# Last batch dense through both experts, first spread ahead of the weight pieces, tile choice and weight fetch ahead of the exponentials

## The reference

```python
x = x + xattn(layernorm(x), ctx, ctx)      # 16 batches of 256 tokens, 256 wide, 16 heads of 16
x = x + ffn(layernorm(x))

# xattn: blocks of 64 keys; every query block of the pattern has a softmax of its own,
# and the outputs of the blocks are added; then @ Wo.T
# ffn:
gate_scores = xf @ gate_w.T                # 2 experts, each token goes to one of them
one_hot = one_hot(argmax(softmax(gate_scores)), 2)
masked = xf[None] * one_hot.T[:, :, None]
h = relu(einsum('end,edh->enh', masked, w1) + b1[:, None, :])      # hidden 1024
expert_out = einsum('enh,ehd->end', h, w2) + b2[:, None, :]
shared = relu(xf @ sw1 + sb1) @ sw2 + sb2
return expert_out.sum(0) + shared
```

## Time and profile before

| | |
|---|---|
| median of 3 executions | 1091.39 us (1087.02 to 1092.59) |
| the profiled execution, own time | 1088.73 us |
| its span, first to last instruction | 1086.9 us |
| granted TensorE clock, mean | 0.924 of full speed |
| busy: PE / PEld | 81% / 68% |
| busy: DVE / POOL / ACT | 49% / 46% / 41% |
| DMA moved | 164.68 MB, mean 152 GB/s |

### The profile page before, as it was taken

One profiled execution on the slowest core, in us unless ns is written; L12 is line 12 of the kernel. 1 busy time (PEld: TensorE's weight loads), 2 busy tenths in 40 slices (PEclk: granted clock), 3 DMA queues, 4 the chain that ended last, 5 costly groups with the idle time before them and its releaser, 6 DMA issues. The chain is left out here.

```text
span 1086.9 us, 21971 instructions
## 1 busy us (share of the span) xinstructions
PE 880.9 (81%) x7654; PEld 734.8 (68%) x7654; DVE 535.5 (49%) x1089; ACT 444.3 (41%) x974; POOL 499.9 (46%) x816
## 2 busy tenths in 40 slices
PE   3377788889888898887998888889888799898564
PEld 2155566777767686776877686868677686768564
DVE  4467473464636464554736364545556373634100
ACT  3151524344444444353443444444445344344232
POOL 7242525154453536262543535363636344457333
PEclk8577887999999999999998999999999999999777
DMA  9666563819284655739192746647382909152740
GB/s 243 152 204 165 175 127 119 202 59 232 43 247 77 202 126 165 163 83 245 43 241 44 240 89 193 135 135 193 93 235 78 250 26 253 42 195 91 278 165 10
DMA packets 95745, 164.68 MB, mean 152 GB/s; under 512 B 9040, under 2 KB 81616, under 8 KB 87008
## 3 DMA queue, kind: packets, MB, share of 16 engines
q1 hardware_dynamic: 75552, 69.80, 29.4%
q10 hardware_dynamic: 9792, 71.31, 18.8%
q0 software_dynamic: 10368, 23.14, 8.4%
HBM read 124.30 MB, written 39.91 MB: 151 GB/s over the span
## 5 line engine op out<-in xcount | busy, mean ns | idle before, releaser
L1285 POOL TENSOR_TENSOR hl<-h,hh 128x256 fp32r<-128x256 f32 x264 | 197.3, 756 | 416.7 <-ACT hh L810 416.7
L990 DVE TENSOR_REDUCE nmax<-work 128x8 f32<-128x512 f32 x256 | 163.8, 684 | 101.5 <-PE work L468 101.5
L789 ACT ACTIVATE PT<-work 128x512 f32<-128x512 f32 x256 | 131.0, 611 | 80.4 <-PE work L483 80.4
L468 PE MATMUL work<-KP,QP 96*128 96x512 f32 x256 | 102.0, 477 | 74.6 <-DMA QP<-scratch_q 64.4
L810 ACT ACTIVATE h<-hid,bias 128x256 f32<-128x256 f32 x144 | 68.6, 476 | 191.1 <-PE hid L428 183.0
L483 PE MATMUL work<-QP,KP 128*128 128x256 f32 x512 | 104.3, 324 | 46.3 <-ACT PT L789 24.5
L996 DVE COPY T<-num 128x512 f32<-128x512 f32 x64 | 44.3, 692 | 189.0 <-PE num L501 189.0
L483 PEld LDWEIGHTS work<-QP,KP 128*128 128x128 f32 x512 | 74.5, 198 | 82.3 <-ACT PT L789 44.0
L428 PE MATMUL hid<-XS,WS 128*128 128x256 f32 x816 | 118.2, 296 | 3.1 <-DVE idle L1158 3.1
L428 PEld LDWEIGHTS hid<-XS,WS 128*128 128x128 f32 x816 | 109.6, 201 | 11.8 <-issue 6.2
L468 PEld LDWEIGHTS work<-KP,QP 96*128 96x128 f32 x256 | 46.3, 211 | 95.5 <-DMA QP<-scratch_q 43.6
(11 more groups left out here) (197 smaller groups left out, 1544.5 us busy)
## 6 DMA issues: line engine op xcount, KB each, us to landing
WR<-wx ACTq DMA_DIRECT2D x64, 1024.0 KB, 10.0
KP<-scratch_k SPq DMA_DIRECT2D x96, 128.0 KB, 12.4
QP<-scratch_q SPq DMA_DIRECT2D x96, 128.0 KB, 13.7
scratch_k<-T SPq DMA_DIRECT2D x16, 512.0 KB, 3.9
scratch_q<-T SPq DMA_DIRECT2D x16, 512.0 KB, 2.9
wx<-WR POOLq DMA_DIRECT2D x16, 512.0 KB, 3.9
stages<-wraw POOLq DMA_DIRECT2D x24, 256.0 KB, 5.7
rowin<-queue SPq DMA_DIRECT2D x16, 260.0 KB
```

The lines of the kernel that those rows point to most:

```text
L468: nc.tensor.matmul(bank, R(QP[0:SHIFT_ROW, p, P * t:P * t + P]), R(KP[0:SHIFT_ROW, p, :, :]), start=True, stop=True).then_inc(sem["s_full" ...
L789: nc.scalar.activation(PT[:, j % 8].rearrange("p t q -> p (t q)"), work[:, BANK[("st", j)], :], ACT.Exp).then_inc(sem["exp_done"], 1)
L990: nc.vector.tensor_reduce(nmax[:, t, 8 * p:8 * p + 8], work[:, BANK[("s", j)], :].rearrange("q (b k) -> q b k", k=BLOCK), AX_X, ALU.max, n ...
L1285: nc.gpsimd.tensor_tensor(R(hl[:, k % 2, a]), h32[:, k % 2, a], hh[:, k % 2, a], ALU.subtract).then_inc(sem["hl_done"], 1)
```

## The change

The queue holds 15 batches instead of 16. The last batch isn't appended: in the tail it goes through both experts whole, once with expert 0's rows kept and once with expert 1's, masked by `last_mask`, and both sums and the shared expert's stay in one PSUM accumulation, added to x1b at the end and stored by SP. In the tail stand now, in units: 1 to 3 of the 14th full tile, 4 of the rest of expert 1 (WX, XL1), 4 of the rest of expert 0 (WR, XL0), 4 of the last batch through expert 0 (WR, XD0), 4 through expert 1 (WX, XD1), 4 through the shared expert (WS, XS). WX is expert 1's weights in buffers that attention no longer needs (KP, QP, wp_hi), fetched by SP once; WR is refilled once with expert 0's. These are six passes: 23 calls of `ffn_up` and 24 of `ffn_down`.

In the loop, PE does `up(6)` behind the third transposed score tile instead of behind the last `values`, `up(7)` ahead of `spread_inverse`, and `down(7)` ahead of `project_out`. ACT fetches the weights ahead of the first exponential, in two DMAs of 2 MB, and does `relu(6)` behind the second group of exponentials. POOL does `update` and `select` ahead of `append`.

At the start, DVE clears QP, V is no longer used for spread_pairs, and POOL issues the pieces from the fifth on only once the first spread has landed.

```diff
-QROWS = BATCH * SEQ
+QROWS = (BATCH - 1) * SEQ
...
+        WX = [KP[:, 0:4].rearrange("p a b c -> p (a b c)"), KP[:, 4:8].rearrange("p a b c -> p (a b c)"),
+              QP.rearrange("p a c -> p (a c)"), wp_hi.rearrange("p a b c -> p (a b c)")]
+        XL1, XL0, XD0, XD1 = (c_hi, c_lo), (a_hi, a_lo), (wp_lo[:, 0], wp_lo[:, 1]), (wp_lo[:, 2], wp_lo[:, 3])
...
-            sp.wait_ge(sem["zeroed"], 7)
+            sp.wait_ge(sem["kp_zeroed"], 1)
+            sp.wait_ge(sem["qp_zeroed"], 1)
             spread(16, "first_q_bounced", "first_k_bounced")
...
             iteration(LAST, False)
-            load_tile(LAST + 1)
-            store(LAST + 1)
-            load_tile(LAST + 2)
+            sp.wait_ge(sem["sel_done"], LAST)
+            sp.wait_ge(sem["rT_full"], LAST - 1)
+            sp.wait_ge(sem["ids_done"], LAST - 1)
+            start = sp.value_load(control[0:1, 0:1], min_val=0, max_val=QROWS - TILE)
+            sp.dma_start(rowin[:, :, :], queue[bass.ds(start, TILE), :].rearrange("(t p) w -> p t w", p=P)) \
+                .then_inc(sem["row_loaded"], 16)
+            sp.wait_ge(sem["st_full"], HEADS * BATCH)
+            load_unit(WX[0], 1, 0, "wx_loaded0")
+            load_unit(WX[1], 1, 1, "wx_loaded0")
+            load_unit(WX[2], 1, 2, "wx_loaded1")
+            sp.wait_ge(sem["wo_full"], BATCH)
+            load_unit(WX[3], 1, 3, "wx_loaded2")
+            for k in range(RU):
+                sp.wait_ge(sem["w2_done"], unit_no(BATCH, k) + 1)
+                load_unit(WR[:, k], 0, k, f"wl_loaded{k}")
+            sp.wait_ge(sem["finished"], TAIL_PASSES[3])
+            sp.wait_ge(sem["routed_out"], 32 * LAST)
+            sp.dma_start(out[LAST].rearrange("(t p) d -> p t d", p=P), x1b[:, :, :]).then_inc(sem["out_done"], 16)
...
+            ffn_up(i, 1)
+            ffn_down(i, 0)
+            tail_tokens(0, xhat, 1)
+            ffn_up(i, 2)
+            ffn_down(i, 1)
+            tail_tokens(1, xin, 2)
...
+            for i in (BATCH + 1, BATCH + 2):
+                for k in range(UNITS):
+                    ffn_up(i, k)
+                    ffn_down(*((i, k - 1) if k else (i - 1, UNITS - 1)))
+            ffn_down(i, UNITS - 1)
...
-                for k in range(RU):
-                    if type(i) is not int or i > 2:
-                        act.wait_ge(sem["w2_done"], unit_no(i, k) + 1)
-                    act.dma_start(WR[:, k].rearrange("p a b c -> p (a b c)"),
+                for h in range(2):
+                    act.dma_start(WR[:, 2 * h:2 * h + 2].rearrange("p k a b c -> p (k a b c)"),
...
+            nc.vector.memset(QP[:, :, :], 0.0).then_inc(sem["qp_zeroed"], 1)
             norm1_stats(0)
...
+            dve.wait_ge(sem["w2_done"], unit_no(BATCH + 2, UNITS - 1) + 1)
+            dve.wait_ge(sem["x1b_done"], BATCH)
+            nc.vector.tensor_tensor(x1b[:, :, :], acc[:, :, :], x1b[:, :, :], ALU.add).then_inc(sem["finished"], 1)
...
-                    append(i - 1)
                     update(i - 1)
                 if type(i) is not int or i >= 2:
                     select(i - 1)
+                if later:
+                    append(i - 1)
...
+            pool.wait_ge(sem["k_spread"], 96)
+            pool.wait_ge(sem["q_spread"], 96)
+            for n in range(4, STAGES + EARLY_PIECES):
+                load(n)
...
+            pool.wait_ge(sem["routed_out"], 32 * (LAST - 1))
+            nc.gpsimd.tensor_copy(ids[:, :], rowin[:, :, D]).then_inc(sem["ids_done"], 1)
             hidden_low(i, 6)
...
             for t in range(TT):
                 pool.indirect_dma_start(out_rows, by_row(ap=ids[:, t:t + 1], axis=0), yr[:, t, :], None,
                                         compute_op=ALU.add).then_inc(sem["routed_out"], 16)
-            pool.wait_ge(sem["routed_out"], 32 * BATCH)
```

More of the change, by code:

```diff
@@ L55, in pass_no @@
     return 0 if type(i) is int and i == 1 else 2 * (i - 2) + (k >= RU)
+TAIL_PASSES = {n: pass_no(BATCH, 0) + n for n in (1, 2, 3)}
 def active(i, k):
@@ L600, in ffn_up @@
+                                       [(hi[:, c, :], lo[:, c, :]) for c in range(DC)])
                 mm.then_inc(sem["hid_full"], 1)
@@ L658, in iteration @@
                     front_project(i + 1, "q", 0, a_hi, a_lo, "xT_lo")
-                for j in range(4):
+                for j in range(3):
                     scores_t(i, j)
+                up(6)
+                scores_t(i, 3)
                 for v in range(VISITS):
@@ L714, in _ @@
-            nc.tensor.matmul(work[:, 1, 2:3], ones16[:, :], mask16[:, 1:2], start=False, stop=True,
-                             skip_group_check=True).then_inc(sem["cnt_full"], 1)
-            ffn_down(i, 2)
-            for k in range(RU, UNITS):
-                ffn_up(i, k)
-                ffn_down(i, k - 1)
-                if k == UNITS - 2:
-                    pe.wait_ge(sem["row_loaded"], 16 * LAST)
-                    transposed(work[:, 2], rowin).then_inc(sem["rT_full"], 1)
-            i = LAST + 2
@@ L735, in _ @@
-            i = LAST + 3
-            for k in range(RU):
-                ffn_up(i, k)
-                ffn_down(*((i, k - 1) if k else (i - 1, UNITS - 1)))
-            ffn_down(i, RU - 1)
+            transposed(work[:, 2], rows).then_inc(sem["x2T_full"], 1)
+            ffn_up(i, 4)
+            ffn_down(i, 3)
+            ffn_up(i, 5)
+            ffn_down(i, 4)
+            tail_tokens(0, ctx_in, 3)
+            ffn_up(i, 6)
+            ffn_down(i, 5)
+            tail_tokens(1, x1, 4)
+            ffn_up(i, 7)
@@ L1222, in _, with tail_low, masked @@
             halves = "p (c t) -> p c t"
-            norm2_apply(LAST)
-            gate_scores(LAST, 0)
-            gate_scores(LAST, 1)
-            choose(LAST)
-            shared_low(LAST, work[:, 0].rearrange(halves, c=2))
-            route(LAST, work[:, 1])
-            finish_routed(LAST + 1)
-            dve.wait_ge(sem["upd_done"], BATCH)
+            def tail_low(n, bank, dst):
+                low(n - 1, "tail_hi", work[:, bank].rearrange(halves, c=2), dst[0][:, :, :], dst[1][:, :, :], "tail_lo")
+            def masked(dst, src, which, e):
+                for t in range(TT):
+                    last = nc.vector.tensor_scalar(dst[:, t, :], src[:, t, 0:D], which[:, e, t:t + 1], None, ALU.mult)
+                last.then_inc(sem["tail_masked"], 1)
+            dve.wait_ge(sem["upd_done"], LAST)
             dve.wait_ge(sem["sel_done"], LAST)
@@ L1242, in _ @@
                 .then_inc(sem["left_step"], 1)
[L1243 to L1245 removed]
+            dve.wait_ge(sem["row_loaded"], 16 * LAST)
             dve.wait_ge(sem["left_step"], 4)
[L1247 to L1251 removed]
@@ L1523, in _ @@
             iteration(LAST, False)
-            i = LAST + 1
+            pool.wait_ge(sem["row_loaded"], 16 * (LAST - 1))
+            pool.wait_ge(sem["wr_loaded1"], 16 * (LAST - 1))
+            nc.gpsimd.tensor_copy(control[:, 0:1], head0[:, :]).then_inc(sem["sel_done"], 1)
+            i = BATCH
             reciprocal_deviation(LAST, 1)
-            hidden_low(i, 1)
+            for k in range(1, 4):
+                hidden_low(i, k)
             add_bias(LAST)
-            hidden_low(i, 2)
-            hidden_low(i, 3)
-            append(LAST)
-            update(LAST)
-            select(LAST)
             hidden_low(i, 4)
@@ L1561, in _ @@
                                         compute_op=ALU.add).then_inc(sem["routed_out"], 16)
-            pool.wait_ge(sem["routed_out"], 32 * BATCH)
+            for k in range(RU + 1, UNITS):
+                hidden_low(i + 1, k)
+            for k in range(UNITS):
+                hidden_low(i + 2, k)
 def kernel(**inputs):
```

271 lines of the change are left out of this document (128 added, 143 removed).

## The result

| | median of the runs, us | lowest to highest |
|---|---|---|
| before | 1091.99 | 1087.02 to 1100.73 (4 runs) |
| changed | 1113.03 | 1108.92 to 1115.21 (4 runs) |

The ratio is 1.020, its 95% interval 1.015 to 1.025: slower by 2%, where 990 us were forecast with a range to 1035. In some executions a kernel runs in a slower state, and runs over 1.5% above the fastest of the same kernel are left out of every median and ratio here. The profiled execution has a span of 1107.1 us against 1086.9.

The account below looks back on a forecast made before the run. PE and its wait for the spread, held up by the weight fetch, were taken to bound the loop. Loop -55 - 36 + 17 = -74, start -5, tail -19 from 1086.9, plus 1.8 outside: 991, stated as 990 us, range 962 to 1035.

Parts of the forecast that it names:

- (a): Loop: ACT issues the weight fetch 7.4 us sooner, so the spread needs its own time only; 55 us saved.
- Both losses, 43 and 12 us: Loop: PE's waits for the spread over 13 iterations, 43 us, and lower granted clock in six windows, 12 us; both go.
- R1: Rival, loop: the fetch collides with the row queue, rows land at 675 and the spread wait returns; 1029 us, chance 0.14.
- R4: Rival, loop: appended rows hold SP's one queue, the spread is issued 4.0 us later; 1123 us, chance 0.04.
- R5: Rival, loop: late control keeps the fetch from getting ahead; (b) lost, (a) half; 1038 us, chance 0.05.
- The rule that I held against (c): Loop DMA: engines alternate queues by packet, so appended rows would be in only with the weights, at 675.
- (c): Loop: rows appended later delay SP's tile fetch and PE's rowin; costs 1.3 us an iteration, 17 us, bounds 0 and 52.
- The chance of 0.05 for slower: Whole kernel: chance that the change makes it slower, from R4 at 0.04 and a little of mixtures.
- (b): Loop: up(6) among the transposed scores, up(7) and up(0) farther down, fill PE's waits; 2.4 us an iteration, 36 us saved.
- the layout by hand: Loop: PE's schedule with exponentials of 0.51 us; the last den group ends at 676.35 with up(6) done, 2.0 us gained.
- The start: Before the loop: fewer weight pieces issued into the first spread; 5 us saved, first scores at 31 to 35.
- The tail: Behind the loop: units, waits and the end take 87 us against 106; 19 us saved, bounds 8 and 27.

Follow-up runs that it names:

- e9: Changed kernel with the weight fetch at the same place, as four 1 MB transfers in 8 KB pieces instead of two of 2 MB in 16 KB; 1032.2 us.
- e1: Changed kernel with the weight fetch issued behind the first four exponentials instead of ahead of them; 1031.7 us, ratio 0.946 to before.
- e7: Changed kernel with the weight fetch issued behind one exponential instead of ahead of the first; 1017.9 us.
- e8: Changed kernel with the same two 2 MB weight transfers issued by SP behind its store of q, in one queue, instead of by ACT; 1013.1 us.
- e3: Changed kernel with the weight fetch at the same place, as four 1 MB transfers in 4 KB pieces instead of two of 2 MB in 16 KB; 1029.8 us.
- e11: Changed kernel with q's parts in their own tile instead of T's first half, four staging buffers instead of six, and an added ACT wait; 1033.9 us.
- e4: Kernel before with only its four 1 MB weight transfers moved ahead of the first exponentials; 1114.9 us, ratio 1.022 to before.
- e13: e7 with up(6) and its relu put back behind the products, as before the change; 1033.8 us.
- e2: Changed kernel with the weight fetch back at the third visit, its place before the change; 1097.8 us, ratio 1.005 to before.
- e14: e7 with append again ahead of update and select on POOL, as before the change; 1049.5 us.
- e15: e7 with the weight fetch of iteration 2 alone moved behind four exponentials; 1023.2 us.

## Why the prediction was wrong

**The step that failed.** Term (a) followed the fetch forward in time and asked what it would meet: the exponentials, the spread, the tile, the rows. It never asked what it would land on. "The weights are issued at 662.5" stands in the forecast; the kernel before issued its store of q at 662.10 in that iteration, so the two were 0.4 us apart on paper, with no row in the text for that store. In the changed kernel both follow the same copy of q and are 0.06 to 0.18 us apart, where at 0.34 to 0.37 us the store still lands in under 5 (table above). The sum also had the cut of the fetch as nothing but 0.47 us an issue; with the four transfers of the kernel before at the same place (e9) it takes 1032.2 us. "Both losses, 43 and 12 us, go" came true for the first: the spread's DMAs land 5.0 and 8.1 us after issue (forecast 6 to 9) and PE's wait for it is 2.5 us in the loop. In its place came the wait for T, 94.0 us of PE in 11 iterations, and the low clock, 0.92 to 0.95 in the windows of these. e1, e7 and e8 (fetch 1 to 3 us later, in e8 in the store's queue too: minus 81, 95 and 100 us), e3 and e9 (only the cut of the fetch: minus 83 and 81) and e11 (the tile and the waits for it: minus 79) show it from three sides.

**The rivals.** R1 and R4 had the right kind of mechanism, small rows beside large ones, on the wrong victim. R4's number, 1123, is near the result by accident: its mark, the spread issued late because of the rows, is not what bounds the changed kernel, where SP's spread waits for TensorE in 13 cases. R5 is what e4 shows, in the kernel before without the new order on POOL. The rule that I held against (c), turns between queues, spoke against (a); I applied it to one small transfer and not to all that are in flight at that moment. The chance of 0.05 for slower was far too small for an edit that puts 4 MB at a new place.

**(b)**, forecast at 36 us, is worth 11 to 16 (e13, up to 22 by the periods) where the fetch is out of the way, and 3 beside e1's fetch, which cannot be told from nothing; in e2, where the spread binds, it bought nothing. Of the 4.0 us of waiting an iteration that the layout by hand counted on, PE had 24.5 / 15 = 1.6 us as waits in the earlier trace rows; the rest I had taken for waits "between matmuls" without a row.

**(c)**, forecast at 17 us: in e7 PE waits 3.2 us for rowin and 23.5 - 14.9 = 8.6 us for the spread in the loop, 12 together; in e8 15.1 and 10.4. The size was about right, as waits; what the rows cost in time was not measured by itself. But the edit that has this price also makes control early, which is worth 26 to 32 us once the fetch is ahead (e14).

**The start**, forecast at 5 us: the first scores begin at 33.93, inside the 31 to 35, but by the fourth store of q 1.7 us are left (175.31 against 176.96), and none in e7. **The tail**, forecast at 87 us: 86.87, with one wait of PE of 3.03 us and one of 2.06, and 7.0 us from the last matmul (1100.1) to the end. Right in its parts too.

**The rest.** e7 is 28 us above the forecast. (b) explains 14 to 25 of them and the start 5, (c) gives 5 back, and the one stall left in e7 would be 8; e15 without that stall was not faster, so how these add up is not settled. e15's best period is 54.07, the forecast one; what makes others 58 is a wait of 2.5 us for the spread with a lower clock behind it. Why one iteration falls on this side and the next on the other stays open.

## What to carry to other kernels

When a transfer is moved, list every transfer that is issued within a few microseconds of its new place, with the buffer that each holds and who wants that buffer next; a small store with a reader nearby is the one to look for, not only the loads that the move is meant to help. If two must be issued together, put the small one first and leave a microsecond between them (e7: the store lands in 3.4 us), or cut the large one in smaller pieces (e3: 5.7). Moving the large one into the small one's queue went with the best time here, but it also came 1.9 us later, so the queue by itself is not shown. A wait that is removed by an edit may have been what kept two things apart: here early control was good, the fetch ahead was good, and together they cost more than both gave.

## What the runs showed of the hardware

A store of 512 KB in pieces of 1 KB lands in 2.9 us alone and in 15.0 to 16.3 beside a fetch of 4 MB in pieces of 16 KB from another queue, if that fetch comes up to 0.19 us behind it; at 0.34 us and more it lands in under 5, with all the 4 MB beside it. No store with such pieces lay between 0.19 and 0.34 us. With smaller pieces the delay fades: 12.9 to 8.0 us between 0.11 and 0.26 us at 8 KB, 6.5 to 4.4 between 0.16 and 0.26 at 4 KB. The Trainium skill (DMA: Bandwidth & Descriptors, section Queues, rings and completion order) says that an engine drains a packet of some 9 to 17 descriptors from one queue before it turns to another. By that figure a store of 512 pieces over 16 engines, 32 on each, is an estimated two to four such packets, each of which can have a turn of the fetch ahead of it, and a turn of larger pieces is longer. The table agrees in direction: beside pieces of 16 KB the store landed behind the whole fetch (625.2 and 624.8 in the iteration shown), beside smaller ones sooner. A turn that is always a whole transfer does not fit, since e9 and e3 both have transfers of 1 MB and at the same distance land the store in 11.2 to 12.2 and 6.0 to 6.5 us. The expectation of e3 took a packet for one piece, which that figure does not say. No run here shows the turns themselves, or why the edge is so sharp.

PE's clock fell where PE stood: 1.00 ahead of the stand of 8.63 us, 0.64 in it, 0.79 in the ten microseconds behind it. In e7 and e8 the mean over the last eleven iterations, all without that stand, is 1.00.
